# Gather with side-by-side table parts and picks as rows; feed-forward steps moved within a pass

## The reference

```python
# layer 1, experts (X normalised)
logits = sigmoid(einsum('bth,eh->bte', X, Wr))
topk_vals, topk_I = top_k(logits.transpose(0, 2, 1), 64)
Xg = take_along_axis(X, idx_flat[:, :, None], axis=1)      # rows of the picked tokens
Q = concatenate([rope(Q[..., :64], topk_I), Q[..., 64:]])  # K in the same way
M = topk_I[..., :, None] >= topk_I[..., None, :]
AV = softmax(where(M, scores, -inf)) @ V * topk_vals[..., None]
out = zeros.at[batch, idx_flat].add(AV @ Wo)
# layer 2, feed-forward (x normalised)
x + (silu(x @ w_gate.T) * (x @ w_up.T)) @ w_down.T
```

## Time and profile before

| | before |
|---|---|
| median of 3 runs | 1512.54 us (1510.91 to 1514.23) |
| the profiled execution | 1513.41 us, span 1511.6 us |
| PE busy | 1455.2 us (96%) |
| DVE busy | 834.9 us (55%) |
| ACT busy | 745.4 us (49%) |
| mean granted clock of TensorE | 0.993 |

### The profile page before, as it was taken

How to read it: one execution, slowest core, us unless ns; L and a number is a source line. 1 busy time by engine, 2 the same in 40 slices (tenths; PEclk the granted TensorE clock), 3 DMA queues, 4 the chain that set the end, 5 groups by cost and what they waited for, 6 DMA issues and landing times.

```text
span 1511.6 us, 25351 instructions
## 1 busy us (share of the span) xinstructions
PE 1455.2 (96%) x8470; PEld 864.9 (57%) x8470; DVE 834.9 (55%) x1521; ACT 745.4 (49%) x1170; POOL 45.1 (3%) x41
## 2 busy tenths in 40 slices
PE   6989899999999999999999999999999999999977
PEld 2676555555556555655555555655556556555544
DVE  8768633455555556455545555455555555555547
ACT  4346545555544554455545545455545544455521
POOL 5000400000000000000000000000000000000000
PEclk9999999999999999999999999999999999999989
DMA  6002100000000000000000000000000000000000
GB/s 203 1 14 72 31 7 1 1 8 1 1 1 10 8 1 1 10 8 1 1 9 9 1 1 1 10 7 1 1 10 8 1 1 2 10 1 1 1 7 8
DMA packets 24096, 17.91 MB, mean 12 GB/s; under 512 B 1632, under 2 KB 22240, under 8 KB 23936
## 3 DMA queue, kind: packets, MB, share of 16 engines
q1 hardware_dynamic: 23600, 14.27, 3.4%
q0 software_dynamic: 336, 1.64, 0.3%
HBM read 11.70 MB, written 4.19 MB: 11 GB/s over the span
## 4 chain that ended last, share of the span: by engine, by line
issue 85%; DVE 2%; PE 1%; POOL 1%; ACT 0%; POOLq 0%; DVEq 0%
PE psum L1182 1%; DVE arena L874 0%; DVE arena L872 0%; DVE arena L880 0%; POOL v_w_hl L573 0%; POOL u_w_hl L573 0%; DVE arena L897 0%; POOL rstd_s L588 0%; DVE xn_s L628 0%; PE psum L1509 0%; POOL u_w_hl L570 0%; POOL up_hl L573 0%; POOL v_w_hl L570 0%; DVE x_all L890 0%; POOL gate_hl L570 0%
## 5 line engine op out<-in xcount | busy, mean ns | idle before, releaser
L1116 ACT ACTIVATE arena<-psum 128x1024 f32<-128x1024 f32 x504 | 475.6, 1031 | 597.3 <-PE psum L1182 595.9
L1182 PE MATMUL psum<-arena 128*64 128x512 f32 x2016 | 460.4, 598 | 1.6 <-ACT arena L1116 1.6
L1182 PEld LDWEIGHTS psum<-arena 128*64 128x64 f32 x2016 | 133.7, 136 | 250.4 <-issue 245.8
L1182 PE MATMUL psum<-v_parts,u_parts 64*128 64x512 f32 (+1 forms) x1568 | 203.2, 398 | 1.9 <-DVE o_hl L825 1.9
L1182 PE MATMUL psum<-u_parts,v_parts 64*128 64x512 f32 x1536 | 196.4, 399 | 5.1 <-issue 4.4
L823 DVE TENSOR_SCALAR o_hl<-psum,sums 128x512 fp32r<-128x512 f32 x126 | 94.5, 750 | 178.1 <-PE psum L1182 178.1
L1182 PEld LDWEIGHTS psum<-v_parts,u_parts 64*128 64x128 f32 (+1 forms) x1568 | 144.9, 184 | 83.7 <-issue 51.1
L1182 PEld LDWEIGHTS psum<-u_parts,v_parts 64*128 64x128 f32 x1536 | 139.5, 184 | 85.5 <-issue 43.9
L980 ACT ACTIVATE arena<-psum 128x512 f32<-128x512 f32 (+3 forms) x186 | 105.9, 609 | 65.7 <-PE psum L1182 46.9
L825 DVE SCALAR_TENSOR_TENSOR o_hl<-psum,sums,o_hl 128x512 fp32r<-128x512 f32 x126 | 94.6, 751 | 4.5
L737 DVE CAST u_parts<-arena 128x512 fp32r<-128x512 f32 x64 | 28.4, 443 | 120.0 <-ACT arena L1059 120.0
(11 more groups left out here) (215 smaller groups left out, 1613.0 us busy)
## 6 DMA issues: line engine op xcount, KB each, us to landing
x_all<-in_x SPq DMA_DIRECT2D x4, 512.0 KB, 5.7
upper<-in_we SPq DMA_DIRECT2D x8, 256.0 KB, 2.7
expert_rows<-upper SPq DMA_DIRECT2D x16, 128.0 KB, 2.5
xn_s<-expert_rows SPq DMA_DIRECT2D x8, 256.0 KB, 2.8
out<-x_all SPq DMA_DIRECT2D x8, 256.0 KB, 2.8
arena<-in_e POOLq DMA_DIRECT2D x1, 896.0 KB, 5.1
arena<-in_wi POOLq DMA_DIRECT2D x1, 576.0 KB, 5.6
uT_w<-in_uT SPq DMA_DIRECT2D x1, 512.0 KB, 6.5
```

Source lines behind the costliest of these rows:

```text
L1116: nc.scalar.activation(th_of(un), psum[:, at:at + 2], ACT.Tanh, scale=0.5 * FACTOR_SCALE ** 2).then_inc(s_th, 2)
L1182: return nc.tensor.matmul(out, lhsT, rhs, start=start, stop=stop)
```

## The change

Gather: the table holds only cosines and sines (64 columns), and its high and low parts stand side by side in one stationary tile of 128 columns, so that four matmuls give 128 rows, the parts of cosine and sine. ScalarE copies them (`turns`), and one matmul with a constant matrix `join` adds the parts and lays the four groups out. For the picks the 18 value columns are stationary and the selections move; the result, 18 rows of 512, is copied by ScalarE (`rows_of_picks`) and transposed in four pieces into bank 7. VectorE makes the values of all batches once, the selections of a batch in one instruction, and no copies of ranks, means and deviations per batch. For the first batch the low rows are made before the ranks are there, the selections signal block by block, and TensorE does the rows first; for the others it does turns, picks, rows, join, transposes. ScalarE's order for a batch is turns, rows of picks, the cast of the next batch's rows, and the three copies. The loops over the batches are written out.

Second layer: gate and up of the second part move from half 9 to 6, those of the third from 13 to 9, and down from 15 to 12; the tail's order follows. ScalarE's copy of y in the tail comes at `den` instead of `down`.

```diff
-FULL_STEPS = {1: [("back", 0)], 2: [("norm", 0)], 3: [("kq", 0), ("v", 0)], 15: [("down", 0), ("den", 0), ("yo", 0)]}
-FULL_STEPS |= {h: [("gate", f), ("up", f)] for h, f in ((5, 0), (9, 1), (13, 2))}
+FULL_STEPS = {1: [("back", 0)], 2: [("norm", 0)], 3: [("kq", 0), ("v", 0)], 12: [("down", 0)], 15: [("den", 0), ("yo", 0)]}
+FULL_STEPS |= {h: [("gate", f), ("up", f)] for h, f in ((5, 0), (6, 1), (9, 2))}
...
-        mr_s = sb("mr_s", [P, 2, 2, TB])
...
-        rk_s = take(2, TB, E)
...
-        table = take_upper(TB, P)
+        table, joined = take_upper(TB, NROT), take_upper(P)
...
-        table_hl = picked_hl[:, 0]
-        values_hl = [picked_hl[:, 1, par, 0:TB * NPICK].rearrange("p (k c) -> p k c", k=TB) for par in range(2)]
+        table_hl = picked_hl[:, 0, 0].rearrange("p (k c) -> p k c", k=TB)
+        turned = picked_hl[:, 0, 1]
+        per_pick = picked_hl[:, 1].rearrange("p a t -> p (a t)")
+        values_hl = per_pick[:, 0:B * TB * NPICK].rearrange("p (b k c) -> p b k c", b=B, k=TB)
+        join = per_pick[:, B * TB * NPICK:B * TB * NPICK + P]
+        pick_rows = [u_raw0[0:NPICK], v_raw0[0:NPICK]]
...
+        s_sel0, s_tab, s_tabc = sem("first_sel_ready"), sem("turns_gathered"), sem("turns_copied")
+        s_pick, s_pickc = sem("picks_gathered"), sem("picks_copied")
...
-        phase_consts = [(table, io["table"].rearrange("(k p) c -> p k c", p=P)),
+        phase_consts = [(table, io["table"].rearrange("(k p) c -> p k c", p=P)), (joined, io["joined"]),
...
-            def first_norm(n, par):
-                nc.vector.tensor_copy(mr_s[:, par, 0], mv1[:, n, :, 0])
-                link(nc.vector.tensor_copy(mr_s[:, par, 1], rstd1[:, n]))
-                return normalised(xn_g[:, par], n, mr_s[:, par, 0].unsqueeze(2), mr_s[:, par, 1].unsqueeze(2))
...
-            link(nc.vector.tensor_copy(table_hl[:, 0], table[:].rearrange("p k c -> p (k c)")))
-            for par in range(2):
-                nc.vector.tensor_copy(values_hl[par][:, :, 0:2], token_at.unsqueeze(2).broadcast_to([P, TB, 2]))
-            nc.vector.tensor_tensor(table_hl[:, 1], table[:].rearrange("p k c -> p (k c)"), table_hl[:, 0], ALU.subtract)
+            nc.vector.tensor_copy(join, joined[:])
+            link(nc.vector.tensor_copy(table_hl[:, :, 0:NROT], table[:]))
+            nc.vector.tensor_tensor(table_hl[:, :, NROT:], table[:], table_hl[:, :, 0:NROT], ALU.subtract)
+            for n in range(B):
+                nc.vector.tensor_copy(values_hl[:, n, :, 0:2], token_at.unsqueeze(2).broadcast_to([P, TB, 2]))
...
+            def low_rows(n, par):
+                dve.wait_ge(s_xgh, n + 1)
+                return nc.vector.tensor_tensor(xn_hl[:, par, 1], xn_g[:, par].rearrange("p k d -> p (k d)"), xn_hl[:, par, 0], ALU.subtract)
+            low_rows(0, 0)
+            low_rows(1, 1)
-            def gather(n, par):
-                if later(n):
-                    dve.wait_ge(s_gath, n - 1)
-                nc.vector.tensor_copy(values_hl[par][:, :, 2:2 + E], value_of[:, :, :, n])
-                ranks = nc.vector.tensor_copy(rk_s[:, par], rank_of[:, :, :, n])
-                if later(n):
-                    first_norm(n, par).then_inc(s_xg, 1)
-                else:
-                    link(ranks)
-                xn = xn_g[:, par].rearrange("p k d -> p (k d)")
-                nc.vector.tensor_tensor(values_hl[par][:, :, 2 + E:], value_of[:, :, :, n], values_hl[par][:, :, 2:2 + E], ALU.subtract)
-                for k in range(TB):
-                    ins = nc.vector.tensor_tensor(sels[par][:, k].rearrange("p (e q) -> p e q", e=E),
-                                                  rk_s[:, par, k].unsqueeze(2).broadcast_to([P, E, KSEL]),
-                                                  iota1.unsqueeze(1).broadcast_to([P, E, KSEL]), ALU.is_equal)
-                dve.wait_ge(s_xgh, n + 1)
-                nc.vector.tensor_tensor(xn_hl[:, par, 1], xn, xn_hl[:, par, 0], ALU.subtract).then_inc(s_sel, 1)
-            gather(0, 0)
-            gather(1, 1)
-            loop(1, B // 2, 2, lambda m: [gather(m * 2 + par, par) for par in range(2)])
+            def selections(n, par, blocks):
+                return nc.vector.tensor_tensor(sels[par][:, blocks].rearrange("p k (e q) -> p k e q", e=E),
+                                               rank_of[:, blocks, :, n].unsqueeze(3).broadcast_to([P, blocks.stop - blocks.start, E, KSEL]),
+                                               iota1.unsqueeze(1).unsqueeze(1).broadcast_to([P, blocks.stop - blocks.start, E, KSEL]),
+                                               ALU.is_equal)
+            for k in range(TB):
+                selections(0, 0, slice(k, k + 1)).then_inc(s_sel0, 1)
+            for k in range(TB):
+                ins = nc.vector.tensor_copy(values_hl[:, :, k, 2:2 + E], value_of[:, k].rearrange("p e b -> p b e"))
+            link(ins)
+            for k in range(TB):
+                ins = nc.vector.tensor_tensor(values_hl[:, :, k, 2 + E:], value_of[:, k].rearrange("p e b -> p b e"),
+                                              values_hl[:, :, k, 2:2 + E], ALU.subtract)
+            ins.then_inc(s_sel, 1)
+            selections(1, 1, slice(0, TB)).then_inc(s_sel, 1)
+            for n in range(2, B):
+                par = n % 2
+                dve.wait_ge(s_gath, n - 1)
+                normalised(xn_g[:, par], n, mv1[:, n, :, 0:1], rstd1[:, n].unsqueeze(2)).then_inc(s_xg, 1)
+                selections(n, par, slice(0, TB))
+                low_rows(n, par).then_inc(s_sel, 1)
...
+            def turns(n):
+                act.wait_ge(s_tab, n + 1)
+                copy(turned, bank[6][:]).then_inc(s_tabc, 1)
+            def rows_of_picks(n, par):
+                act.wait_ge(s_pick, n + 1)
+                copy(pick_rows[par], bank[4 + par][0:NPICK]).then_inc(s_pickc, 1)
-                copy(picks[:, n], bank[4 + par][:, 0:(E // 2) * NPICK]).then_inc(s_gx, 1)
-            lagged(fori_of(act), lambda n, par: high_part(n, par) if later(n) else None, picked)
+                copy(picks[:, n], bank[7][:, 0:(E // 2) * NPICK]).then_inc(s_gx, 1)
+            def gathered(n, par):
+                turns(n)
+                rows_of_picks(n, par)
+                if not (isinstance(n, int) and n in (0, B - 1)):
+                    high_part(n + 1, 1 - par)
+                picked(n, par)
+            pairs(fori_of(act), gathered, 2)
...
-                        if step == ("down", 0):
+                        if step == ("den", 0):
...
+            def gather_rows(n, par):
+                for k in range(TB):
+                    if not after_first(n):
+                        pe.wait_ge(s_sel0, k + 1)
+                    for h in range(2):
+                        ins = mm(bank[par][:], xn_hl[:, par, h, k * P:(k + 1) * P], sels[par][:, k], k == h == 0, k == TB - 1 and h == 1)
+                return ins
+            def gather_turns(par):
+                for k in range(TB):
+                    ins = mm(bank[6][:], table_hl[:, k], sels[par][:, k], k == 0, k == TB - 1)
+                ins.then_inc(s_tab, 1)
+            def gather_picks(n, par):
+                for k in range(TB):
+                    ins = mm(bank[4 + par][0:NPICK], values_hl[:, n, k], sels[par][:, k], k == 0, k == TB - 1)
+                ins.then_inc(s_pick, 1)
+                if not after_first(n):
+                    gather_rows(n, par)
-                for out, parts in ((bank[par], xn_hl[:, par]), (bank[2 + par], table_hl)):
-                    for k in range(TB):
-                        for h in range(2):
-                            mm(out[:], parts[:, h, k * P:(k + 1) * P], sels[par][:, k], k == h == 0, k == TB - 1 and h == 1)
+                gather_turns(par)
+                gather_picks(n, par)
+                if after_first(n):
+                    gather_rows(n, par)
+                pe.wait_ge(s_tabc, n + 1)
+                mm(bank[2 + par][:], join, turned)
+                pe.wait_ge(s_pickc, n + 1)
+                if after_first(n):
+                    pe.wait_ge(s_gx, n)
-                    for k in range(TB):
-                        ins = mm(bank[4 + par][:, e2 * NPICK:(e2 + 1) * NPICK], sels[par][:, k, e2 * P:(e2 + 1) * P],
-                                 values_hl[par][:, k], k == 0, k == TB - 1)
+                    ins = nc.tensor.transpose(bank[7][:, e2 * NPICK:(e2 + 1) * NPICK], pick_rows[par][:, e2 * P:(e2 + 1) * P],
+                                              ident[0:NPICK, 0:NPICK])
-            pairs(fori_of(pe), gather)
+            for n in range(B):
+                gather(n, n % 2)
...
-        "table": np.concatenate([cos, cos, -sin, sin], axis=1),
+        "table": np.concatenate([cos, sin], axis=1),
+        "joined": np.tile(np.kron(np.array([[1, 1, 0, 0], [0, 0, -1, 1]]), np.eye(half)), (2, 1)).astype(np.float32),
```

## The result

| | before | after |
|---|---|---|
| median | 1512.86 us (1510.91 to 1514.23) | 1499.27 us (1498.35 to 1501.55) |
| runs | 4 | 4 |
| the profiled execution | 1513.41 us, span 1511.6 | 1498.35 us, span 1496.6 |

A forecast was written before the change was run, and what follows sets the result against it. TensorE was taken to bound gather and passes, VectorE and then a serial chain the tail. Savings of 7.7 + 3.6 + 0.4 + 4.4 = 16.1 us gave 1497.3 for the profiled execution, 1496.4 as median; range 1493.5 to 1503.

The forecast's parts named there:

- likeliest case: Whole kernel: all four terms come as forecast, 1496.4 us, with its own range of 1494 to 1499; chance 68%.
- rival B: Tail gives only 2 us: down stalls VectorE or the last chain's clock is low; sum 13.7, 1498.8; chance 14%.
- Gather, steady batches: Gather from its second batch on: TensorE's batch falls from 5.50 to 4.40 us, 7.7 us saved in seven.
- rival A: Gather bound by hand-offs, join or transposes waiting for ScalarE: period 5.2 us, sum 10.5, 1502.0; chance 12%.
- VectorE with under 0.2 us of idle time: Sign for the gather: VectorE nearly always busy, with TensorE's batches starting 4.3 to 4.5 us apart.
- Rival D: Gather: one-instruction selection runs at half rate, VectorE's batch 6.5 us, gather loses 7, total 1511; chance 3%.
- First batch: Gather's first batch: ends at 55.4 instead of 59.03 us, 3.6 us saved, taking full clock.
- no half clock at 53: Sign for the gather's first batch: no half-clock stretch there, and the batch done 3.6 us earlier.
- Passes: The seven main passes: steps only move between halves, net -0.06 us a pass, 0.4 us saved in seven.
- Tail: Second layer of the last batch alone: store issued at 1504.4 instead of 1508.91, 4.4 us saved.
- 0.2 of small waits: Tail: allowance for VectorE's waits before its last large operation, D6, which moves it from 1499.72 to 1499.9.
- stall of 0.7: Tail: VectorE waits 0.7 us for down at half clock (4.54 us), made into some 2 by A6's rows behind it.

The follow-up runs named there:

- before_again: The kernel before, unchanged, run and profiled once more: 1511.69 us, ratio 0.9993.
- gather_only: The kernel before with the new gather alone; gate, up and down stay in their old places: 1499.77 us, ratio 0.9918.
- no_low_rows: The changed kernel without TensorE's four matmuls per batch for the rows' low parts, so it computes less than it should: 1503.26 us, ratio 0.9946.
- after_again: The changed kernel, unchanged, run and profiled once more: 1497.65 us, ratio 0.9906 against the kernel before.
- steps_only: The kernel before with the old gather and only the new places of gate, up and down: 1510.51 us, ratio 0.9987.
- down_15: The changed kernel with down put back in half 15, gates and ups moved as in the change: 1497.22 us, ratio 0.9908.
- fill_end: The changed kernel with 10 unread matmuls on TensorE before the last y round of the tail: 1497.99 us, ratio 0.9900.
- fill_all: The changed kernel with unread matmuls in the tail: 18 before norm, 5 before kq, 10 before the last y round: 1497.01 us, ratio 0.9896.

## Why the prediction was right, and where its terms were off

The measured 1499.27 lies inside the range, 2.9 above the forecast, and just outside the 1494 to 1499 of the likeliest case. The gather and the halves of a pass came as the likeliest case had them. The tail came as rival B, which had 14%: it gave 2.2, with both of B's reasons in it, and B's sum of 13.7 and its 1498.8 are closer to the measured 13.6 and 1499.27 than the forecast is. That the sum came out between the two is in part luck: the passes gave 1.7 us that no term had, and 3.1 us of the gap between the two profiles are half-clock stretches of the one of before.

**Gather, steady batches: right.** Forecast 4.40 us, measured 4.46 to 4.51; 7 x 1.02 = 7.1 instead of 7.7. By terms: turns and picks 1.96 (1.96 forecast), rows 1.83 to 1.87 (1.86), join 0.32 (0.24), transposes 0.35 (0.44 less 0.1). TensorE is the bound, with nothing idle, and both hand-offs are covered, so rival A is out. Wrong was the mark "VectorE with under 0.2 us of idle time": it idles 0.54 to 0.59. I counted its start 0.29 us after the batch and a signal of 0.11 besides; it starts 0.11 after the batch, since it waits for the transposes that stand just before. The merged selection took 2.28, 2.21 from its start to that of the low rows, where I put 2.17. Rival D, half rate for the merged selection, would have made it twice that.

**First batch: right in place, small in worth.** Forecast done at 55.4, measured 55.69. The working let the selections start at 48.30 and they started at 48.63; from there the batch took 7.06 us, where the working has 7.1. The set-up, counted at nothing, doesn't show: the ranks came at 48.2 to 49.1 us in the profiles with the new gather and at 48.3 to 48.65 in those with the old. The idle time before turns and picks was 0.58 where the working had 0.4, and the transposes waited 0.41 where it had some 0.6. The "no half clock at 53" came true too, but not for the reason given: before_again has no such stretch either, with the same idle time. So of the 3.3 us only some 1.8 are the change's; the other 1.5 the profile of before had by chance. The forecast took the half clock of one profile for the kernel's: its 11.3 for the gather stand against 10.4 between the profiles of before and after, and 8.9 between before_again and gather_only.

**Passes: right in the halves, too small in sum.** Half 6 became 1.45 us longer and half 13 1.47 shorter, half 12 2.67 longer and half 15 2.70 shorter, -0.05 in sum where -0.06 was forecast. Between before and after no other half changed by more than 0.1. Yet the seven passes gave 2.1, not 0.4. One kernel's passes differ by 1.1 to 1.5 from one execution to another, so a part of this can be chance; but in the table the three profiles with the old steps have 1155.5 to 1157.9, those with the gates and ups moved, no_low_rows aside, 1153.1 to 1154.7. Some of the difference lies at the boundary of a pass, in the gap before the first scores, which the profile calls issue: 0.69 us in the mean of six in before, 0.65 in before_again, 0.58 in after, 0.44 in after_again, but 0.68 in gather_only, 0.49 in steps_only and 0.65 in down_15. Between before and after that is 0.7 of the 2.1 us. Since no_low_rows showed 7.5 us there from no change in the passes at all, I can't say whether the rest is the moved steps or where the program came to stand. It stays open; the old steps with unread matmuls ahead of the loop would be the test, and it wasn't run.

**Tail: mechanism right, term too large by 2.2.** Forecast 4.4, measured 2.2. D6 was to come 2.2 us later and came 3.3 later: the three evacuations are the 2.07 that were counted, and the "0.2 of small waits" were two stalls of 0.53 (VectorE before gate 1, for ScalarE's tanh) and 0.60 (before A6, whose rows stand on TensorE behind down's 24 matmuls). The second is the "stall of 0.7" that the working had seen for half clock only. The last chain then took 5.73 instead of 4.32, since its clock was low: 1.4. Together 2.4, less some 0.2: the working puts the store at 1504.4, where its own 1499.9 and 4.32 make 1504.2, and takes off 0.1 more for a signal. This is rival B; its price was 2, and it came. The argument against it, that TensorE had kept its full clock from 1477 to 1497 while idle for 3 of 20 us, didn't carry: in after it idled 2.4 of 12.5 us before the fall, a little more, and 1.5 of it in one piece just ahead of the last chain. A row of a denser stretch can't speak for a thinner one.

And 1.6 of the 2.2 that the tail did gain is that down ran at half clock in the profile of before and not in before_again. Against before_again the tail gains 0.6 (steps_only, with the old gather, has the same 52.65), against gather_only 0.2; those two have the same tail, and differ by 0.4 in VectorE's wait before the last gate, 0.86 and 0.47 us. The 2.1 us by which the median of steps_only is lower are for passes and tail together.

## What to carry over

Where matmuls have few moving columns and a new stationary tile each, swap the operands so that the many columns move, even if small transposes are needed afterwards: it paid 0.3 us in a batch of 5.5, and high and low parts joined in one stationary tile paid most of the other 0.7. In a serial tail, don't clear the last chain of its dense matmuls, since the full clock can go with them: with down back at the end the tail was 1.3 us shorter. Before a forecast is made from one profile, ask of each half-clock stretch in it whether a second profile has it too: two that a second one hadn't were 3.1 of the 15.1 us here.

## What the runs showed of the hardware

- Short half-clock stretches of 3.4 us come in one execution and not in the next: before had one at 53.4, after_again one at 153.5, fill_end at 95.4 and 170.5, fill_all at 94.8 and 169.9, steps_only at 98.7 and 180.7, and after, gather_only and down_15 none before the tail. They follow places where TensorE idles: it was busy for 1.4 of the 3.4 us ahead of that of before, for 1.7 in after_again, 1.4 and 1.5 in fill_end, 2.1 and 1.5 in steps_only. The idle time alone doesn't decide it, since before_again was busy for 1.5 of 3.4 us at the same place and stayed at full clock. The one at 53.4 cost 1.5 us, the two of fill_end 1.8 together, the one of after_again 0.4. The first of fill_end, in windows (columns as above):

```profile
92.00:95.42 3.42, 1.38 (x13) 1.19 (x12) 2.40 (x4) 1.30 (x3) 0.00 (x0) 1.00 0.23 77
95.42:98.80 3.38, 3.38 (x7) 1.47 (x6) 2.85 (x5) 1.38 (x7) 0.00 (x0) 0.50 0.00 0
```

- In the tail 23 matmuls of 512 columns in idle places cut a half-clock stretch of 17 us to 3.4 and the tail by 2.1 us, with no work taken away.
- A run of matmuls without any wait can stop for 1.0 us in each pass of a loop, in one program and not in another, with the same instructions in the loop. With 32 matmuls fewer ahead of the loop it stopped, with 32 small ones put back it didn't, worth 7.5 us in seven passes.
